# Overlapping ranges of segment sums, added in two halves, and x's part of the last layer in other steps of the head

## The reference, cut to what matters

```python
msg_in = concat([x[src], x[dst]])                      # 100000 x 256
h = relu(msg_in @ Wm1 + bm1)
h = relu(h @ Wm2 + bm2)                                # 100000 x 256
messages = h @ Wm3 + bm3
agg = segment_sum(messages, dst) / clip(count, 1)
upd = relu(concat([x, agg]) @ Wn1 + bn1) @ Wn2 + bn2
out = layernorm(x + x + upd)
```

## Time and profile before

| | |
|---|---|
| median of 3 runs | 1233.46 us |
| the profiled execution's own time | 1233.96 us |
| its span | 1230.5 us |
| TensorE busy | 1185.1 us (96%) |
| VectorE busy | 933.7 us (76%) |
| GpSimd busy | 774.7 us (63%) |
| ScalarE busy | 746.9 us (61%) |
| granted TensorE clock, mean | 0.992 |

### The profile page before, as it was taken

The page is one execution under the profiler, slowest core; times in us unless marked ns, Lnnn a source line. Parts: engine busy times, 40 slices in busy tenths (PEclk is TensorE's granted clock), DMA queues, the critical chain, the costliest instruction groups (busy, mean ns, idle before and its releaser), DMA issues.

```text
span 1230.5 us, 32746 instructions
## 1 busy us (share of the span) xinstructions
PE 1185.1 (96%) x9782; PEld 1164.4 (95%) x9783; DVE 933.7 (76%) x2021; ACT 746.9 (61%) x1405; POOL 774.7 (63%) x811
## 2 busy tenths in 40 slices
PE   6878999999999999999999999999999999999996
PEld 5767999999999999999999999999999999998886
DVE  6755877777877877777778777887877787777675
ACT  3445666666666666656666666666666666564786
POOL 2066777777777777767777777777777777772000
PEclk9898999999999999999999999999999999999998
DMA  9774666656666666656556566566666666553022
GB/s 327 272 274 140 180 179 177 178 174 180 175 177 179 178 173 175 173 171 174 171 172 176 172 175 175 171 174 172 172 172 170 173 171 175 164 168 104 21 75 90
DMA packets 135604, 211.39 MB, mean 172 GB/s; under 512 B 24248, under 2 KB 102670, under 8 KB 134031
## 3 DMA queue, kind: packets, MB, share of 16 engines
q1 hardware_dynamic: 98030, 108.43, 29.3%
q0 software_dynamic: 37536, 102.55, 29.1%
HBM read 188.09 MB, written 22.80 MB: 171 GB/s over the span
## 4 chain that ended last, share of the span: by engine, by line
PE 87%; DMA 3%; DVE 3%; issue 2%; POOL 2%; SPq 2%; ACT 1%; DVEq 1%
PE bank L1324 42%; PE bank L1293 13%; PE sums L1251 8%; PE sums L1253 8%; PE bank L1234 7%; PE bank L1356 3%; POOL a_edge L589 2%; PE sums L1369 2%; DMA a_edge<-a_table,src_idx 1%; DMA b_win<-b_table 1%; PE bank L1146 1%; PE bank L1341 1%; PE bank L1134 1%; PE sums L1134 1%; PE bank L1352 0%
## 5 line engine op out<-in xcount | busy, mean ns | idle before, releaser
L589 POOL DMA_INDIRECT a_edge<-a_table,src_idx x782 | 754.0, 964 | 288.6 <-issue 143.6
L1324 PE MATMUL bank<-w,h 128*128 128x256 f32 x4692 | 618.3, 281 | 0.0
L1324 PEld LDWEIGHTS bank<-w,h 128*128 128x128 f32 x4692 | 582.1, 188 | 0.0
L683 ACT ACTIVATE h_hi<-bank 128x512 fp32r<-128x512 f32 x391 | 234.2, 599 | 367.9 <-PE bank L1324 363.2
L969 DVE SCALAR_TENSOR_TENSOR onehot<-iota,first_node,dst_col 128x256 fp32r<-128x256 int16 x439 | 209.0, 483 | 113.2 <-issue 80.8
L1040 DVE SCALAR_TENSOR_TENSOR h<-bank,h 128x512 fp32r<-128x512 f32 x391 | 265.8, 680 | 7.0 <-ACT h L693 5.4
L1034 DVE SCALAR_TENSOR_TENSOR h_lo<-bank,h_hi 128x512 fp32r<-128x512 f32 x391 | 266.4, 681 | 0.7 <-ACT h_hi L683 0.7
L690 ACT COPY bank<-b_bc 128x512 f32<-128x512 f32 x391 | 232.2, 594 | 28.0 <-DVE h_lo L1034 24.3
L1293 PE MATMUL bank<-ident,a_edge 128*128 128x128 f32 x1564 | 236.2, 274 | 6.5 <-DVE onehot_t L954 6.5
L693 ACT ACTIVATE h<-bank 128x512 fp32r<-128x512 f32 x391 | 233.1, 596 | 5.5 <-PE bank L1234 2.7
L1251 PE MATMUL sums<-h_hi,onehot 128*128 128x258 f32 x878 | 233.2, 287 | 0.4 <-DVE h_lo L1034 0.4
(11 more groups left out here) (174 smaller groups left out, 540.4 us busy)
## 6 DMA issues: line engine op xcount, KB each, us to landing
b_win<-b_table SPq DMA_DIRECT2D x391, 128.0 KB
rel<-rel_dram SPq DMA_DIRECT2D x196, 128.0 KB, 3.4
a_edge<-a_table,src_idx POOLq DMA_INDIRECT x782
a_table<-work SPq DMA_DIRECT2D x12, 512.0 KB, 4.6
b_table<-work SPq DMA_DIRECT2D x5, 1024.0 KB, 5.9
b_table<-h SPq DMA_DIRECT2D x4, 1024.0 KB, 5.7
f_x<-in_x SPq DMA_DIRECT2D x12, 256.0 KB, 5.2
b_table<-a_edge SPq DMA_DIRECT2D x3, 1024.0 KB, 5.0
```

What stands on the lines that cost most here:

```text
L589: pool.indirect_dma_start(a_edge[:, b % R * TB + t, :], None, a_table, bass.IndirectOffsetOnAxis(ap=src_idx[:, b * TB + t:b * TB + t + 1], ...
L683: act.activation(h2_hi[:, (k - AHEAD - 1) % U, :, 0:H], bank[H2[(k - AHEAD - 1) % U]][:, :].rearrange("p (t h) -> p t h", t=TB), ACT.Relu) ...
L1324: ins = pe.matmul(to, h1[:, j, a, h * EB + t * P:h * EB + (t + 1) * P], w2[:, b, h, :], start=False, stop=(a == 1 and h == KH - 1), skip_g ...
```

## The change

Ranges replace windows: a range starts at a multiple of 96 nodes and is 128 nodes wide, so that neighbours overlap by 32, and a block belongs to the range in which its lowest node lies (edges are compared with their place modulo 128). A block of which some nodes lie beyond its range would be summed further, as before. Counted from dst as the reference draws it: with windows 48 of the 391 blocks lie in two; with ranges none lies outside its own. There are 65 ranges, so 65 ends, where there were 49; the first are 50, 20, 15 and 13 blocks long; behind block 200 there are 8 ranges of five blocks, 21 of four and 16 of three, beside a few of six.

A range starts on any multiple of 32 nodes, so its bank is added to two neighbouring rows of tiles of agg with two masks, from_quarter and to_quarter: once in the step in which the range's last block is summed, once a step later. TensorE begins each range with a matmul that overwrites (start=True) in the other bank, so nothing is cleared; its branch for that stands beside the first matmul of every block's sum.

In the head, x_groups does x's products in steps 5 to 12 (two groups in steps 5 and 8), which leaves three for the end, one of them in banks 2 and 3. The five bank-writing matmuls become one, ScalarE waits for its own copies instead of them, TensorE waits for the zeroed bank only ahead of the first sum. In the first body SyncE loads b_win without waiting for the gather, and VectorE waits for it instead. Making the edges relative to their range moves from GpSimd (one operation) to VectorE (dst_place in step 2, three operations in step 4).

```diff
-        agg = sb("agg", [P, NW * HC], F32)
+        agg = sb("agg", [P, (NW + 1) * HC], F32)
+        from_quarter = sb("from_quarter", [P, P // QUARTER], F32)
+        to_quarter = sb("to_quarter", [P, P // QUARTER], F32)
...
+        TWICE = (XA, XA + 3)
         def x_groups(g):
-            return list(range(NG - 1 - LAG, NG)) if g == NG else [g - 1 - LAG] if g > LAG else []
+            done = max(g - XA, 0) + sum(XA <= t < g for t in TWICE)
+            return list(range(done, NG if g == NG else min(done + 1 + (g in TWICE), NG))) if g >= XA else []
+        X_LAST = [NG - 1, NG - 2, NG - 3]
+        def x_banks(k):
+            return (2, 3) if k == NG - 2 else (6, 7)
...
-                        sp.wait_ge(s_g[k % R], nth(i, k, 16 * TB))
+                        if not isinstance(i, int) or i > 0:
+                            sp.wait_ge(s_g[k % R], nth(i, k, 16 * TB))
                         sp.dma_start(b_win[:, k % RB, :].bitcast(F32),
...
-            act.wait_ge(s_bits, 5)
+            act.wait_ge(s_hxa, 2 * NG)
...
             def first_and_last():
                 dve.wait_ge(s_efd, 1)
+                dve.tensor_single_scalar(dst_place[0:BG, :, :].rearrange("p g e -> p (g e)"),
+                                         edges_in[0:BG, 0:GR * EB], P - 1, ALU.bitwise_and).then_inc(s_wrap, 1)
...
             def make_relative():
...
+                dve.tensor_tensor(dst_range[0:BG, :, :], dst_f,
+                                  first_start[0:BG, :].unsqueeze(2).to_broadcast([BG, GR, EB]), ALU.subtract
+                                  ).then_inc(s_wrap, 1)
+                dve.wait_ge(s_wrap, 2)
+                dve.tensor_single_scalar(dst_range[0:BG, :, :], dst_range[0:BG, :, :], 7, ALU.arith_shift_right
+                                         ).then_inc(s_wrap, 1)
+                dve.wait_ge(s_wrap, 3)
+                dve.scalar_tensor_tensor(rel_win[0:BG, :, :], dst_range[0:BG, :, :], float(P), dst_place[0:BG, :, :],
+                                         ALU.mult, ALU.add).then_inc(s_rel, 1)
...
+            def half_of(which, start, j, half):
+                quarter = within(start & 3, 0, 3)
+                w = within((start >> 2) + j, 0, NW - 1)
+                mask = (from_quarter, to_quarter)[half]
+                return agg[:, bass.ds((w + half) * HC, HC)], bank_at(which), mask[:, bass.ds(quarter, 1)]
+            def add_half(in_agg, at, mask):
+                return dve.scalar_tensor_tensor(in_agg, at, mask, in_agg, ALU.mult, ALU.add)
+            def end_range(i, k, word):
+                start = word & 255
+                dve.reg_mov(left, start)
+                first = half_of(own, start, 0, 0)
+                dve.wait_ge(s_sg, i * U + (k + 1))
+                dve.wait_ge(s_add, added)
+                add_half(*first)
+                further = (word >> 16) & 63
+                with dve.If(further > 0):
...
+                dve.reg_mov(swap, own)
+                dve.reg_mov(own, other)
+                dve.reg_mov(other, swap)
+            def end_second_half():
+                add_half(*half_of(other, within(dve.snap(left), 0, 255), 0, 1)).then_inc(s_add, 1)
                 dve.reg_add(added, added, 1)
-                in_agg = agg[:, bass.ds(w * HC, HC)]
-                dve.tensor_tensor(in_agg, bank_at(which), in_agg, ALU.add).then_inc(s_add, 1)
...
-                    dve.wait_ge(s_add, added)
-                    dve.nop().then_inc(s_fin, 1)
...
-                    with dve.If(word > 2**6 - 1):
+                    with dve.If(word > 2**8 - 1):
+                        if there(i, k - BACK - 1):
+                            with dve.If(word > 2**22 - 1):
+                                end_second_half()
                         if there(i, k - BACK):
-                            end_window(i, k - BACK, word)
-                        if there(i, k - AHEAD - 1):
-                            with dve.If(word > 2**21 - 1):
-                                make_further_onehot(i, k - AHEAD - 1, 1)
+                            with dve.If((word & 2**8) > 0):
+                                end_range(i, k - BACK, word)
...
+            def begin_range(k):
+                pe.wait_ge(s_add, ended)
                 pe.reg_add(ended, ended, 1)
-                sum_further(k)
                 pe.reg_mov(own, other)
                 pe.reg_sub(other, both, own)
+                first_sum(bank_at(own), k % U, k, True)
...
-                    with pe.If(word > 0):
+                    with pe.If((word & (2**13 - 1)) > 0):
...
                     if there(i, k - BACK):
                         pe.wait_ge(s_h2l[(k - BACK) % U], nth(i, k - BACK))
-                        sum_segments(bank_at(own), (k - BACK) % U, k - BACK, False).then_inc(s_sg, 1)
+                        if there(i, k - BACK - 1):
+                            with pe.If(word > 2**13 - 1):
+                                begin_range(k - BACK)
+                            with pe.If(word < 2**13):
+                                first_sum(bank_at(own), (k - BACK) % U, k - BACK, False)
+                        else:
+                            first_sum(bank_at(own), (k - BACK) % U, k - BACK, False)
+                        other_sums(bank_at(own), (k - BACK) % U, k - BACK).then_inc(s_sg, 1)
```

298 lines of the change are left out of this document (156 added, 142 removed).

## The result

Four runs of the changed kernel: median 1222.99 us (1219.12 to 1223.60). The kernel before beside them: 1233.32 (1232.51 to 1233.88). Ratio 0.9912, 95% interval 0.9893 to 0.9931, measured again later as 0.9898 (0.9880 to 0.9915). The change is worth 10.3 us; I had forecast 24.5. The time lies in my range (1200 to 1228), but under half of the gain came, so the forecast is wrong in size and the question is where 14 us went.

A forecast was written before the change was run, and what follows sets the result against it. TensorE's own work was taken to bound the loop, at 2.57 us per block. 1233.96 - 23.0 (sums) - 8.5 (head) + 7 (VectorE) + 0.5 (end) = 1209.96, stated as 1209 us, range 1200 to 1228.

The forecast's parts named there:

- part 3: Branches on TensorE ahead of each block's sum: 0.28 us more sequencer time per block, hidden; 0 taken, bounds 0 and 109.
- Part 4's cover: VectorE in the loop: 0.48 us free per block, so a range of n blocks gives back 0.48n against its end's work.
- Part 4's price and its number: VectorE's extra work at range ends: 2.0 us per end taken, at most 3.15; 7 us in all, bounds 0 and 61.
- Rival B: Gather ring becomes the bound in the loop; half of the 23.0 turns into waits for b_win: 1221 us, chance 0.08.
- Rival A: VectorE becomes the bound in the second half, at 2.4 us per end: 1227 us, chance 0.17.
- My sign for being wrong: TensorE's waits behind onehot_t reaching 30 us would show the prediction wrong; some 10 were expected.
- Part 1: Sums on TensorE: the four further matmuls of 48 twice-summed blocks go, 23.0 us gained.
- Part 2: TensorE's wait in begin_range for the previous range's second-half addition: satisfied two blocks (5 us) early, cost 0.
- Part 5: Head to loop: fewer x groups and bank writes at the end let gathers run on, 8.5 us gained, bounds 5 and 11.
- Part 6: End of the kernel: the last range's second half is added one step later, +0.5 us, from 0 to 1.5.

The follow-up runs named there:

- the loads apart: Changed kernel, but SyncE issues b_win without waiting for the block's gathers in every body and VectorE waits for both transfers: 1202.88 us, ratio 0.9749.
- the repeated run: Changed kernel unaltered, measured and profiled again: 1222.34 us against 1234.28 for the kernel before, ratio 0.9898.
- gap filled: Changed kernel plus eleven unused 512-column products on TensorE behind the last body: 1401.48 us against 1403.11 for the kernel before, ratio 0.9992.
- the operations later and the gap filled as well: The loads apart plus the eleven filling products, VectorE's three edge operations moved from step 4 to 6; first of three runs 1398.85 us against 1403.04, 0.9966.

## Why the prediction was wrong

- **The step that failed** is part 3: "So 0.28 us more is hidden even with a lead near zero", a term of 0. The gap of a quarter us shows in 32 periods, 8.3 us, which is most of the 9 us that the loop lost beyond the forecast. The 0.5 us by which the sequencer was ahead of the transposes was read in a block whose onehot_t was early. Where it is late, transposes and branch start together (834.39), and then 0.89 us of sequencer time stand against 0.67 of matmuls. One branch more in each step cost another 6.9 us.
- **Part 4's cover** is why the case arises at all: "2.57 - 1.86 - 0.23 = 0.48 us per block is free. A range of n blocks gives back 0.48n." The free time is there, but VectorE can save up little of it: it is spent waiting for b_win (66.1 us before, 43.8 after), since b_win is issued behind the gather and the gather behind TensorE. The lead so capped is 1.3 us at the median and 2.2 at most, and a burst of 4.43 us asks for 4.43 - 2.57 = 1.86. Taking that one wait away brings both losses to nil; what each would be without the other is not shown.
- Part 4's price and its number held: the two steps of an end hold VectorE 4.43 + 2.25 - 2 x 1.86 = 2.96 us beyond two plain blocks, 2.04 without the 0.92 of the body's turn, and I took 2.0. Late onehot_ts cost 9.8 us (18.1 - 8.3), and I had 7 beside the 2 that the kernel lost already. That the number came so near is partly luck, since the reason given for it, the saved lead, is what failed.
- **Rival B** named the ring and b_win and gave 1221, at a chance of 0.08, and the measured 1223 is near it. Half of that is luck: the ring was not the bound, the waits of TensorE have no entry for a gather, and the waits for b_win fell; their harm was to hold VectorE's lead down. I had argued against it from GpSimd's issue rate and from stretches at 2.57 us, neither of which shows a capped lead: it costs nothing until a burst comes.
- **Rival A**, VectorE as the bound, predicts a number near it (1227) by the wrong cause: VectorE is busy 78% and with the loads apart loses nothing.
- My sign for being wrong, 30 us of waits behind onehot_t, did not come: the view has 6.7 us from 257 to 1090. The loss stood beside it, as "issue" ahead of the first sum and in periods that are long without a wait in the list.
- **Part 1** held: 192 matmuls and 48 one-hots are gone. **Part 2** held: begin_range's wait shows in no list.
- **Part 5** was mis-sized by 2 (6.5 for 8.5): GpSimd's pause behind the eighth gather went as said (the issue-to-issue 1.26 us runs on), but the first gather came at 80.83, 2.07 later. I had put the 4.8 us of new operations under VectorE's wait of 5.45; that wait stood in a later step, behind the split of x on which the products and so the tables hang. Three of the four stand here ahead of that split (L950), in the repeated run:

```profile
26.14 1.22 DVE L838 TENSOR_TENSOR agg<-agg 98x1024 int32<-98x1024 f32 x1
27.40 0.69 DVE L842 TENSOR_SCALAR agg<-agg 98x1024 int32<-98x1024 int32 x1
28.12 1.23 DVE L845 SCALAR_TENSOR_TENSOR agg<-agg 98x1024 f32<-98x1024 int32 x1
29.27 0.68 DVE L950 TENSOR_TENSOR h<-bank,h 128x512 fp32r<-128x512 f32 x1
```

- **Part 6** was mis-sized: 0.5 forecast and 3.7 measured. With the clock up (gap filled) the end is 0.9 us longer than before (105.7 and 104.8), of the order forecast. The other 2.8 are the low clock, which the prediction did not think of. It is partly the luck of the execution, since the old gap of 2.57 us had it in one of three.
- Added up against the 24.0 forecast between the two profiled executions: the loop 9.0 us less, the head 2.0, the end 3.2, and 1.7 more around the span give the 11.5 measured.

The fastest version run is the one with the loads apart, 0.9749 of the kernel before (0.9715 to 0.9783). The one with the operations later and the gap filled as well was never run under the conditions of the 1234 us; there its head and tail should give some us more, which is not shown.

## What to carry to other kernels

Free time on an engine covers bursts only as far as the engine can run ahead: before counting 0.48 us per block as cover, look in its waits for a transfer that comes just in time, and for what that transfer's issue waits. Two loads that one instruction needs should not be chained on the issuing queue only to save a wait. What a sequencer does behind a wait is hidden only while the wait is satisfied early, so control has to be priced for the case in which it is late. And whether a test did what it was meant to do has to be read in its own trace: one here moved the exposed branches behind another wait, and one added a single branch where two were written; by the totals alone both would have been read the wrong way.

## What the runs showed of the hardware

- The same chip ran the kernel before in 1403 us and, some four minutes later, in 1234 us. In the slower runs GpSimd stands between its gathers for something that no record names, here in the run with the gap filled:

```profile
POOL a_edge L620 <- remote: 280.1, 229, 2.1
POOL a_edge L620 <- issue: 168.1, 545, 0.6
...
POOL a_edge L620 <- PE bank L1355: 7.1, 7, 1.3
```

  The gathers themselves take the same 0.96 us; a block takes 3.09 us on average, and taking b_win out of the ring helps nothing (from block 12 to the last 1170 us without it, 1169 with it). What slows them is open.
- A compare-and-branch on TensorE is 0.20 to 0.21 us when its body is skipped and 0.07 when entered (the added one that is never entered 0.17); on VectorE it is 0.04 to 0.06. The Trainium skill, "Advanced Engine Details and Errata", section Control Flow Timing, gives about 108 ns for one; no row here shows that number, and the measured ones decide.
- TensorE's granted clock fell to the lower level in all eleven executions with an idle stretch of 2.9 to 3.05 us behind the last body, and in one of three with a stretch of 2.57 us at the same place. The lower level lasted 3.4 to 10.2 us and cost up to 3.5 us (tails of 104.8 and 108.3). The Trainium skill, "TensorE: Matmul & The Clock Gate", section "Part 1: The HAM clock gate", has the two levels of 1.2 and 2.4 GHz and says that how busy the engine has been recently sets which. The rows agree in the levels (0.51 and 0.99) and in that each drop here stands behind idle time.
- An idle time that the profile puts down to PE's sums (28.9 us ahead of L1046) was the sequencer's control in the stretch looked at: the sums had ended 1.7 us before the onehot_t that precedes it.
- At the end of a range VectorE stands idle for 1.27 us behind a 0.48 us addition (830.63 to 832.39), when the end is a body's last step: its sequencer is at register operations, two branches and a load of words of 0.34 us. 0.92 of it is the turn of a body that stood there before.
